# One decoder kernel on one core: expert lists exchanged through TensorE, two norms split over two engines, head and tail of the delta rule reordered

## The chip, the cores and the metric

One core of one Trainium2 chip runs the whole program in one launch. The metric is device time in microseconds; the median of three runs of the kernel before is 2662.2 us (2659.61 to 2668.63). All data are float32 unless said.

## What is computed

A decoder of four layers with three sublayers each, every one followed by a layer norm without weights: `x = layernorm(x + f(x))`, with x of 16 sequences x 128 tokens x 256 channels. The change touches three of the twelve sublayers, one after the other in the program:

```python
# third sublayer (L0 ffn): 16 experts share one matrix; each takes its 128 best tokens
S = softmax(xf @ router_w + router_b)              # xf: 2048 x 256
G, idx = top_k(S.T, 128)
out = xf[idx] @ expert_w + expert_b
y = zeros.at[idx].add(G[..., None] * out)
# fourth (L1 attn): gated delta rule, 8 key and 16 value heads of 128
q, k, v, z = split(x @ w_qkvz.T); b, a = split(x @ w_ba.T)
q, k, v = silu(causal_conv4(q, k, v)); q, k = q/|q|, k/|k|
g = -exp(A_log) * softplus(a + dt_bias); beta = sigmoid(b)
for t in tokens:                                   # S: 128 x 128 per head
    S = S * exp(g[t]); S = S + outer(k[t], (v[t] - k[t] @ S) * beta[t]); o[t] = q[t] @ S / sqrt(128)
y = rmsnorm(o * silu(z)) * norm_weight @ w_out.T
# fifth (L1 xattn): WKV scan over time with k = x and v = ctx, per channel
```

## The kernel before

Tokens of a sequence lie on partitions in `x_tok` [128, 16 batches, 256]; `x_chan` is the same turned, channels on partitions. Each sublayer is a block in which every engine has its own instruction list, run in order; semaphores written by hand tie the lists, and a barrier stands between sublayers. PSUM (`banks`) has 8 banks of 512 columns.

**The end of a sublayer.** `dve_stats` takes statistics of a batch once its sum is added. `dve_norm` (lines 145 to 160) aggregates all 16 batches on VectorE, adds epsilon, lets ScalarE take the root (`act_norm`), inverts, and applies the norm to each batch. `pe_turn_x` transposes it in 8 turns of four 128x128 blocks into banks 0 and 1 by turns; `act_turn_x` copies each turn to `x_chan`. Other sublayers already use `dve_moments`, `act_sqrt`, `dve_invert`, `dve_apply` (lines 170 to 197), which do the same for a part of the batches.

**Expert sublayer, `layer0_ffn`.** 2,048 tokens lie in 8 segments of 256, so partition 16 s + e holds the scores of expert e in segment s. Sixteen rounds of a maximum of eight and a replacement give the 128 best of each segment, sorted, in `best`. SyncE writes them to memory and reads them back so that each partition of an expert holds all eight lists (`lists`); VectorE then merges two lists at a time (larger of one and the reversed other) and sorts again, down to the 128th best, from which the gates follow. Then 16 adds with statistics, and the norm.

**Delta rule, `layer1_delta`.** 16 rounds; round i does key head i // 2 for half of the batches. In a round `unit(n)` is the pair of banks 2n and 2n+1. The head, ahead of the rounds: TensorE projects q, k, v of round 0 (`project`), ScalarE copies (`tap`), VectorE convolves in three steps per channel group u (`convolve`; u = 0, 1 keys and queries, 2, 3 values), ScalarE applies SiLU, the norms of k and q go ln, exp to `lengths`. Two things travel through memory: `lengths` to all partitions (`spread_norms`, 4 writes and one broadcast load of 1 MB into `l1a_sq`) and the rows of the decay (`rows_mem`, two writes and one broadcast load of 1 MB a round into `rows`, part of `ctx_tok`). VectorE scans `rows`, ScalarE takes exp, VectorE weighs with beta (`weigh`), giving `e`. In a round: values turned (`turn_values`), k and q scaled by the norms (`normalise`), key products (`multiply_keys`), times e to `aT` and `att`, inverse of the blocks of 16 (`blk`, through memory, then `invert`), merged by doublings on TensorE (e1, e2, xT1, xT2), `solve`, output `o`, gate with `z` (`gate_project`, `z_out`), norm of o (`gate_norm`), turned output, `project_out`, `add`. The output of round i is finished within round i + 1, that of the last behind the loop, together with the layer norm by halves (`layer_norm`). GpSimd squares the keys and makes `al` from `aT`.

**WKV, `layer1_wkv`.** Two channel halves c; the adds of the second go by quads of four batches with statistics, then the norm as above.

## Time and profile before

| what | value |
|---|---|
| median of three runs | 2662.2 us |
| the profiled execution, whole | 2669.9 us |
| its span | 2668.1 us |
| TensorE, VectorE, ScalarE, GpSimd busy | 82%, 68%, 53%, 13% |
| expert sublayer | 252 to 330 us |
| delta rule | 331 to 385 us with its head until about 390, rounds, tail from 1351 to 1385 us |
| WKV | 1386 to 1484 us |

The span is that of one execution; the runs have no profile. In a timeline a line is a group of like instructions on one engine: start, time in us, engine, line, what is written from what, count, and in brackets how long the engine had been idle before and what ended that. SPq is SyncE issuing a DMA: its time is that of the issue, not of the transfer. PEld is the weight load of a matmul. The granted clock is a share of TensorE's full 2.4 GHz; 0.50 is 1.2 GHz.

### The profile page before, as it was taken

To read this page: it belongs to the slowest core of one execution; us is meant where nothing else is said; L and a number is where in the kernel's file an instruction comes from. 1 tells how busy PE (TensorE), PEld (TensorE's weight loads), DVE (VectorE), ACT (ScalarE), POOL (GpSimd) and SP (SyncE) were. 2 spreads that over 40 slices of the span, in tenths; PEclk is the share of its full clock that TensorE was granted. 3 is DMA by queue.
4 is the path that set the end of the run, shared out by engine and by line. 5 is a ranking of instruction groups with operands and counts; after the bars stand their busy time and mean duration, and the time that the engine had idled before them with its cause. 6 is when DMAs were issued, how large, how long until landed. Compare 5 with 4: busy or idle time off the path is not lost. (4 is left out here: it accounts for less than half of the span.)

```text
span 2668.1 us, 45019 instructions
## 1 busy us (share of the span) xinstructions
PE 2193.6 (82%) x18439; PEld 1684.2 (63%) x18439; DVE 1815.3 (68%) x3155; ACT 1408.4 (53%) x2249; POOL 346.8 (13%) x164
## 2 busy tenths in 40 slices
PE   7986268999999999999851697999999756788855
PEld 4665146777777777777740356999998533455633
DVE  5766657888877778888659534444444878688487
ACT  4654146666666666666535323545455346455347
POOL 0000112222322223222200240000000001100201
PEclk9998678999999999999985899999999877999977
DMA  3000021122122212112221462111100000000000
GB/s 144 2 1 13 15 75 52 53 59 58 49 57 62 79 49 58 51 57 54 45 90 47 151 182 73 44 27 47 36 31 0 5 12 0 11 1 1 17 1 32
DMA packets 159506, 122.82 MB, mean 46 GB/s; under 512 B 117728, under 2 KB 145120, under 8 KB 152800
## 3 DMA queue, kind: packets, MB, share of 16 engines
q1 hardware_dynamic: 156256, 116.00, 14.3%
q0 software_dynamic: 3072, 4.33, 0.9%
q8 instruction: 127, 2.08, 0.3%
q14 instruction: 51, 0.42, 0.1%
HBM read 102.62 MB, written 17.66 MB: 45 GB/s over the span
## 5 line engine op out<-in xcount | busy, mean ns | idle before, releaser
L1543 DVE SCALAR_TENSOR_TENSOR ctx_chan<-l1a_raw,l1a_cw,ctx_chan 128x1024 f32<-128x1024 f32 x192 | 230.8, 1277 | 19.7 <-ACT ctx_chan L1394 18.6
L1156 PE MATMUL banks<-x_chan,l1a_wp 128*128 128x512 f32 x512 | 230.5, 604 | 5.2 <-DMA l1a_wp<-in_l1a_wp_dram 5.2
L1120 POOL TENSOR_TENSOR l1a_sq<-ctx_chan 128x1024 f32<-128x1024 f32 x16 | 152.3, 9516 | 356.4 <-ACT ctx_chan L1398 356.4
L1156 PEld LDWEIGHTS banks<-x_chan,l1a_wp 128*128 128x128 f32 x512 | 98.0, 194 | 117.0 <-issue 110.8
L2644 PE MATMUL banks<-x_chan,more_weights_ahead 128*128 (+1 forms) x1024 | 121.1, 277 | 2.1 <-ACT l2a_ready L2500 2.1
L2644 PEld LDWEIGHTS banks<-x_chan,more_weights_ahead 128*128 128x128 f32 x1024 | 119.5, 194 | 3.8 <-issue 1.6
L1193 PE MATMUL banks<-l1a_wo,l1a_oT 128*128 128x256 f32 x512 | 121.1, 385 | 0.0
L1141 POOL TENSOR_TENSOR l1a_al<-l1a_aT,l1a_outer 128x1024 f32<-128x1024 f32 x32 | 74.8, 2358 | 328.6 <-DVE l1a_aT L1603 328.6
L2664 PE MATMUL banks<-l2a_wo,l2a_oT 128*128 128x256 f32 x512 | 113.2, 379 | 0.0
L1164 PE MATMUL banks<-l1a_wz,x_chan 128*128 128x256 f32 x512 | 113.1, 379 | 0.0
L1164 PEld LDWEIGHTS banks<-l1a_wz,x_chan 128*128 128x128 f32 x512 | 97.2, 190 | 19.6 <-issue 7.2
L1392 ACT ACTIVATE l1a_raw<-banks 128x1024 f32<-128x1024 f32 x64 | 65.5, 1023 | 76.9 <-PE banks L1156 76.8
L2664 PEld LDWEIGHTS banks<-l2a_wo,l2a_oT 128*128 128x128 f32 x512 | 96.1, 190 | 12.4
L1193 PEld LDWEIGHTS banks<-l1a_wo,l1a_oT 128*128 128x128 f32 x512 | 94.7, 190 | 13.7
L2509 ACT ACTIVATE l2a_probs<-l2a_masked,l2a_rowmax 128x128 f32<-128x128 f32 x256 | 98.6, 392 | 3.5 <-DVE l2a_rowmax L2551 3.5
L2547 DVE TENSOR_TENSOR l2a_masked<-banks,l2a_maskf 128x1024 f32<-128x1024 f32 x32 | 39.1, 1220 | 83.2 <-PE banks L2652 83.2
L121 PE MATMUL banks<-ident,x_tok 128*128 128x128 f32 x288 | 50.7, 332 | 53.1 <-DVE x_tok L159 26.5
L2571 DVE COPY l2a_vals<-l2a_ready 128x512 f32<-128x512 f32 x16 | 6.8, 427 | 126.8 <-PE banks L2691 116.1
L1726 DVE TENSOR_TENSOR l1a_vt<-banks,l1a_vt 64x512 f32<-64x512 f32 x64 | 44.5, 695 | 69.3 <-PE banks L1222 69.2
L2521 ACT ACTIVATE l2a_probsT<-banks 128x1024 f32<-128x1024 f32 x32 | 32.7, 1023 | 98.9 <-PE banks L2658 98.9
L142 DVE BATCH_NORM_STATS2 ln_stats_buf<-x_tok 128x6 f32<-128x256 f32 x192 | 75.9, 420 | 9.7 <-ACT x_tok L2831 6.5
L1218 PE MATMUL banks<-l1a_vt,l1a_ec 64*64 64x128 f32 x512 | 70.6, 301 | 13.3 <-ACT l1a_ec L1478 13.3
(624 smaller groups left out, 5766.8 us busy)
## 6 DMA issues: line engine op xcount, KB each, us to landing
ctx_tok<-l1a_rows_mem SPq DMA_DIRECT2D x16, 1024.0 KB, 6.7
l1a_sq<-l1a_norm_mem SPq DMA_DIRECT2D x16, 1024.0 KB, 4.5
ctx_chan<-in_ctxT_dram SPq DMA_DIRECT2D x3, 2048.0 KB, 16.9
l1f_wgu<-in_l1f_wgu_dram SPq DMA_DIRECT2D x4, 1408.0 KB, 11.0
moe_sums<-l1x_zero SPq DMA_DIRECT2D x2, 2176.0 KB, 16.5
ctx_tok<-in_ctx_dram SPq DMA_DIRECT2D x2, 2048.0 KB, 11.4
l1a_wp<-in_l1a_wp_dram SPq DMA_DIRECT2D x8, 512.0 KB, 3.6
l1f_wgu<-moe_sums SPq DMA_DIRECT2D x8, 512.0 KB, 8.2
```

Of the source, the lines that this page charges most:

```text
L142: g.nc.vector.bn_stats(g.stats[:, t, :], g.x[:, t, :]).then_inc(ln_stats, 1)
L1120: P.tensor_tensor(sq[:, 0, :], conv[:, 0, :], conv[:, 0, :], ALU.mult).then_inc(s["k_squared"], 1)
L1141: P.tensor_tensor(heads(al, h), heads(aT, h), bc(outer[:], 1, HALF), ALU.mult).then_inc(s["al_made"], 1)
L1156: mm = MM(ps[:, 2 * (u % 2) + q, :], wp[:, c, u * 128:(u + 1) * 128], g.xT[:, c, t0:t0 + 512], start=c == 0, stop=c == 1)
L1164: mm = MM(unit(h)[:, b * 256:(b + 1) * 256], g.xT[:, c, t0:t0 + S], wz[:, c, :], start=c == 0, stop=c == 1)
L1193: mm = MM(unit(h)[:, b * 256:(b + 1) * 256], oT[:, HALF * h + 2 * b + r, :], wo[:, r, :], start=r == 0, stop=r == 1)
L1218: return MM(quarter(q)[0:64, k, :], xT2[0:64, slot, :], vt[0:64, slot, :], start=True, stop=True)
L1392: A(raw[:, u, :, CONV - 1:], now, ACT.Copy)
L1543: V.scalar_tensor_tensor(t, raw[:, u, :, j:j + S], cw[:, c, j:j + 1], t, ALU.mult, ALU.add).then_inc(s["conv_done" if step == 2 else "conv ...
L2509: ins = A(probs[:, k, :], masked[:, k, :], ACT.Exp, bias=rowmax[:, k:k + 1], scale=128 ** -0.5, accum_out=rsum[:, k:k + 1])
L2644: mm = mm_(next_banks(h)[:, k, :], wq[:, c, h * HALF_HEADS + k, :], g.xT[:, c, bass.ts(i, 128)], start=c == 0, stop=c == 1)
L2664: mm = mm_(ps[:, 6, 0:D], oT[:, h, :], wo[:, h, :], start=h == 0, stop=h == HEADS - 1)
```

## The change

In the experts, `best` is transposed once, copied eight-fold to `wide`, and transposed per segment into banks 4 and 5, which gives every partition all eight lists; ScalarE copies every second list to `odd`, and VectorE merges the others with these from PSUM. In the experts and in WKV the norm is made for batches 0 to 7 while the adds of the others run, and ScalarE applies it (`act_apply`). In the delta rule's head the norms are written ahead of the decay rows and loaded ahead of them; `normalise(0)` comes before the scans; gate projection and z of round 0, and SiLU of the values, come ahead of the decay's exponentials; in round 0 the second half of the convolution comes behind the first inverse product. In its tail the gate and output norm come ahead of the first half's layer norm apply and turns, and the output norm uses root and reciprocal by halves instead of ln and exp.

```diff
-def pe_turn_x(pe, g, ready, turned, turned_out, first=0, stop=None):
+def pe_turn_x(pe, g, ready, turned, turned_out, first=0, stop=None, elsewhere=0):
 
     nc = g.nc
     for n in range(first, stop or TURNS) if g.turn_next else ():
         c, t0 = n % DC, n // DC * GROUP
-        pe.wait_ge(ready, t0 + GROUP)
+        pe.wait_ge(ready, t0 + GROUP - elsewhere)
...
+def dve_lower(v, g, s, shift, t0, t1):
+
+    g.nc.vector.scalar_tensor_tensor(shift[:, t0:t1], g.moments[:, t0:t1, 0], -1.0, g.rstd[:, t0:t1], ALU.mult, ALU.mult).then_inc(s["ln_lowered"], 1)
+
+
+def act_apply(act, g, s, shift, t0, t1):
+
+    act.wait_ge(s["ln_lowered"], 1)
+    for t in range(t0, t1):
+        g.nc.scalar.activation(g.x[:, t, :], g.x[:, t, :], ACT.Identity, bias=shift[:, t:t + 1], scale=g.rstd[:, t:t + 1]).then_inc(s["ln_applied"], 1)
...
-            sp.wait_ge(s["best_made"], 1)
-            sp.dma_start(best_mem.rearrange("e (s k) -> s e k", s=SEGS), best[:]).then_inc(s["best_out"], 16)
-            sp.wait_ge(s["best_out"], 16)
-            sp.dma_start(lists[:].rearrange("p s k -> p (s k)"), bc(best_mem, 0, SEGS)).then_inc(s["lists_in"], 16)
...
+            pe.wait_ge(s["best_made"], 1)
+            pe.wait_ge(s["score_out"], 1)
+            nc.tensor.transpose(ps[:, 2, 0:128], best[:], g.ident[:]).then_inc(s["best_turned"], 1)
+            pe.wait_ge(s["wide_made"], 1)
+            pe.wait_ge(s["expert_out"], B // 2)
+            for n in range(SEGS):
+                mm = nc.tensor.transpose(lists[:, n, :], wide[:, n, :], g.ident[:])
+            mm.then_inc(s["lists_made"], 1)
...
-            pe_turn_x(pe, g, s["ln_out"], s["x_turned"], s["x_turned_out"])
+            pe_turn_x(pe, g, s["ln_applied"], s["x_turned"], s["x_turned_out"], stop=TURNS // 2)
+            pe_turn_x(pe, g, s["ln_out"], s["x_turned"], s["x_turned_out"], first=TURNS // 2, elsewhere=EARLY)
...
-            v.wait_ge(s["lists_in"], 16)
-            merge(sort[0][:], lists[:].rearrange("p (n h) k -> p n h k", h=2))
+            v.wait_ge(s["lists_made"], 1)
+            v.wait_ge(s["odd_out"], 1)
+            link(V.tensor_tensor(sort[0][:], lists[:, 0::2, :], odd[:, :, ::-1], ALU.max))
...
+                if i == EARLY:
+                    dve_moments(v, g, s, 0, EARLY)
+                if i == EARLY + 1:
+                    dve_invert(v, g, s, 0, EARLY, 1)
+                    dve_lower(v, g, s, shift, 0, EARLY)
                 v.wait_ge(s["biased"], i // 2 + 1)
                 at = i % 2 * SEGS + i // 2
                 V.scalar_tensor_tensor(g.x[:, i, :], y[:, i, :], wt[:, at:at + 1], g.x[:, i, :], ALU.mult, ALU.add).then_inc(s["added"], 1)
                 dve_stats(v, g, i, (s["added"], i + 1), s["ln_stats"])
-            dve_norm(v, g, s["ln_stats"], s["ln_mean"], s["ln_sqrt"], s["ln_out"], have_stats=True)
+            dve_moments(v, g, s, EARLY, B)
+            dve_invert(v, g, s, EARLY, B, 2)
+            dve_apply(v, g, s, EARLY, B)
...
-            act_norm(act, g, s["ln_mean"], s["ln_sqrt"])
+            act.wait_ge(s["best_turned"], 1)
+            nc.scalar.activation(wide[:].rearrange("p s (a e) -> p s a e", e=ROUTED),
+                                 bc(ps[:, 2, 0:128].rearrange("p (s e) -> p s e", e=ROUTED), 2, SEGS), ACT.Copy).then_inc(s["wide_made"], 1)
+            act.wait_ge(s["lists_made"], 1)
+            nc.scalar.activation(odd[:], lists[:, 1::2, :], ACT.Copy).then_inc(s["odd_out"], 1)
+            nc.scalar.activation(g.scratch[:], g.ones[:, 0:1], ACT.Sqrt)
+            act_sqrt(act, g, s, 0, EARLY, 1)
+            act_apply(act, g, s, shift, 0, EARLY)
+            act_sqrt(act, g, s, EARLY, B, 2)
...
+            def load_rows(i):
+                k = i // 2
+                sp.dma_start(rows, rows_mem[k, i % 2].rearrange("b n -> (b n)").partition_broadcast(128)).then_inc(s["rows_in"], 16)
+
+            def norms_out(i):
+                sp.wait_ge(s["norm_rs"], i + 1)
+                for j in range(4):
+                    sp.dma_start(norm_mem[j:j + 1, :], lengths[32 * j:32 * j + 1, :]).then_inc(s["norm_out"], 16)
+
+            def norms_in(i):
+                sp.wait_ge(s["norm_out"], 64 * i + 64)
+                sp.dma_start(sq[:].rearrange("p u n -> p (u n)"), norm_mem.rearrange("j n -> (j n)").partition_broadcast(128)).then_inc(s["norm_in"], 16)
+
+            norms_out(0)
             sp.wait_ge(s["rows_begun"], 1)
             for h in range(2):
                 sp.dma_start(rows_mem[:, h], turned[:, h, :]).then_inc(s["rows_out"], 16)
+            norms_in(0)
             sp.wait_ge(s["rows_out"], 32)
...
             load_rows(0)
...
-            spread_norms(0)
...
                 if i + 1 < ROUNDS:
-                    spread_norms(i + 1)
+                    norms_out(i + 1)
+                    norms_in(i + 1)
...
                 for h in range(2):
                     pe.wait_ge(s["silu"], 4 * i + 4)
-                    if h == 0:
+                    if i == 0:
+                        pe.wait_ge(s["z_out"], h + 1)
+                    elif h == 0:
                         pe.wait_ge(s["norm_ln"], i + 1)
                     elif i > 1:
                         pe.wait_ge(s["added"], 2 * i - 2)
-                    elif i:
-                        pe.wait_ge(s["z_out"], 2)
-                    else:
-                        pe.wait_ge(s["tap"], 4)
                     turn_values(h)
...
-                pe.wait_ge(s["wz_loaded"], 16 * (i // 2) + 16)
-                for h in range(2):
-                    if more:
-                        pe.wait_ge(s["tap"], 4 * i + 7 + h)
-                    else:
-                        pe.wait_ge(s["oT_out"], 2 * i - 1 + h)
-                    gate_project(i, h)
+                if i:
+                    pe.wait_ge(s["wz_loaded"], 16 * (i // 2) + 16)
+                    for h in range(2):
+                        if more:
+                            pe.wait_ge(s["tap"], 4 * i + 7 + h)
+                        else:
+                            pe.wait_ge(s["oT_out"], 2 * i - 1 + h)
+                        gate_project(i, h)
...
             pe.wait_ge(s["rest_loaded"], 16 * 4)
+            pe.wait_ge(s["wz_loaded"], 16)
+            pe.wait_ge(s["norm_ln"], 1)
+            pe.wait_ge(s["tap"], 4)
+            for h in range(2):
+                gate_project(0, h)
             for i in range(ROUNDS):
                 round_(i)
             pe.wait_ge(s["added"], 2 * ROUNDS - 2)
-            pe_turn_x(pe, g, s["ln_out"], s["x_turned"], s["x_turned_out"], 0, TURNS // 2)
-            pe.wait_ge(s["x_turned_out"], TURNS // 2)
             for h in range(2):
                 pe.wait_ge(s["normed"], 2 * ROUNDS - 1 + h)
                 turn_output(h)
             for h in range(2):
                 pe.wait_ge(s["oT_out"], 2 * ROUNDS - 1 + h)
                 project_out(h)
+            pe.wait_ge(s["added"], 2 * ROUNDS - 1)
+            pe_turn_x(pe, g, s["ln_out"], s["x_turned"], s["x_turned_out"], 0, TURNS // 2)
             pe.wait_ge(s["added"], 2 * ROUNDS)
             pe_turn_x(pe, g, s["ln_out"], s["x_turned"], s["x_turned_out"], TURNS // 2, TURNS)
 
...
-                for h in range(2):
-                    z_out(i, h)
-                if more:
-                    for u in range(2):
-                        silu(i + 1, u)
+                if i:
+                    for h in range(2):
+                        z_out(i, h)
+                    if more:
+                        for u in range(2):
+                            silu(i + 1, u)
                 act.wait_ge(s["e1_made"], i + 1)
                 A(ec[:], compact(2), ACT.Copy).then_inc(s["e1_out"], 1)
                 act.wait_ge(s["e1T_made"], i + 1)
                 A(ecT[:], compact(3), ACT.Copy).then_inc(s["e1T_out"], 1)
+                if i == 0:
+                    for u in range(2):
+                        silu(1, u)
...
             act.wait_ge(s["gates_turned"], 1)
             A(turned, ps[:, 5, 0:256].rearrange("p (a n) -> p a n", a=2), ACT.Copy).then_inc(s["gates_out"], 1)
             for h in range(2):
-                decay_exp(0, h)
+                z_out(0, h)
             for u in range(2, 4):
                 silu(0, u)
+            for h in range(2):
+                decay_exp(0, h)
             for i in range(ROUNDS):
                 round_(i)
             act.wait_ge(s["ln_mean"], NB + 1)
             A(g.rstd[:, 0:NB], g.rstd[:, 0:NB], ACT.Sqrt).then_inc(s["ln_sqrt"], 1)
-            act_turn_x(act, g, s["x_turned"], s["x_turned_out"], 0, TURNS // 2)
             for h in range(2):
                 square(ROUNDS - 1, h)
-            gate_norm(ROUNDS - 1)
+            for h in range(2):
+                now = slice(HALF * h, HALF * h + HALF)
+                act.wait_ge(s["gsum"], 2 * ROUNDS - 1 + h)
+                A(rs[:, now], ss[:, now], ACT.Sqrt, scale=1.0 / 128, bias=eps[:, 0:1]).then_inc(s["g_rs"], 1)
             for h in range(2):
                 output_turned(ROUNDS - 1, h)
-            A(g.scratch[:], g.ones[:, 0:1], ACT.Sqrt)
+            act_turn_x(act, g, s["x_turned"], s["x_turned_out"], 0, TURNS // 2)
             act.wait_ge(s["ln_mean"], 2 * NB + 3)
             A(g.rstd[:, NB:B], g.rstd[:, NB:B], ACT.Sqrt).then_inc(s["ln_sqrt"], 1)
             act_turn_x(act, g, s["x_turned"], s["x_turned_out"], TURNS // 2, TURNS)
...
             def round_(i):
                 more = i + 1 < ROUNDS
-                for u in range(2):
-                    normalise(i, u)
-                if i:
+                if i:
+                    for u in range(2):
+                        normalise(i, u)
                     for h in range(2):
                         gate(i - 1, h)
                     v.wait_ge(s["al_made"], 2 * i)
...
                 if more:
                     for h in range(2):
                         scan(i + 1, h)
-                    for first in (0, 2):
+                    for first in (0, 2) if i else (0,):
                         for step in range(3):
                             convolve(i + 1, first, step)
                 v.wait_ge(s["e1_out"], i + 1)
                 V.tensor_tensor(p1[:], ec[:], bc(fold[:], 1, VH), ALU.add).then_inc(s["p1_made"], 1)
                 if i:
                     add(i - 1, 0)
+                else:
+                    for step in range(3):
+                        convolve(1, 2, step)
                 v.wait_ge(s["e2_made"], i + 1)
                 V.tensor_tensor(p2[:], compact(2), bc(fold[:], 1, VH), ALU.add).then_inc(s["p2_made"], 1)
                 if more:
...
                 convolve(0, 2, step)
             v.wait_ge(s["rest_loaded"], 16 * 4)
             v.wait_ge(s["zeroed"], 3)
+            for u in range(2):
+                normalise(0, u)
             for h in range(2):
                 scan(0, h)
             for h in range(2):
...
                 round_(i)
             last = ROUNDS - 1
 
-            def layer_norm(half):
+            def layer_norm(half, apply_now):
 
                 done = (NB + 2) * half
                 batches = range(NB * half, NB * half + NB)
...
                 V.tensor_scalar(g.rstd[:, now], g.moments[:, now, 1], 1e-5, None, ALU.add).then_inc(s["ln_mean"], 1)
                 v.wait_ge(s["ln_sqrt"], half + 1)
                 V.reciprocal(g.rstd[:, now], g.rstd[:, now]).then_inc(s["ln_mean"], 1)
-                v.wait_ge(s["ln_mean"], done + NB + 2)
-                for t in batches:
+                if apply_now:
+                    apply(half)
+
+            def apply(half):
+                v.wait_ge(s["ln_mean"], (NB + 2) * half + NB + 2)
+                for t in range(NB * half, NB * half + NB):
                     V.tensor_scalar(g.x[:, t, :], g.x[:, t, :], g.moments[:, t, 0:1], g.rstd[:, t:t + 1],
                                     ALU.subtract, ALU.mult).then_inc(s["ln_out"], 1)
 
-            layer_norm(0)
+            layer_norm(0, False)
             for h in range(2):
                 gate(last, h)
             for h in range(2):
                 sum_gated(last, h)
             for h in range(2):
-                scale_gated(last, h)
+                now = rs[:, HALF * h:HALF * h + HALF]
+                v.wait_ge(s["g_rs"], ROUNDS + h)
+                V.reciprocal(now, now).then_inc(s["g_inverted"], 1)
+                v.wait_ge(s["g_inverted"], h + 1)
+                V.tensor_tensor(heads(go, h), heads(go, h), bc(now, 2, 128), ALU.mult).then_inc(s["normed"], 1)
+            apply(0)
             for h in range(2):
                 add(last, h)
-            layer_norm(1)
+            layer_norm(1, True)
...
+                if n == QUADS + 1:
+                    dve_moments(v, g, s, 0, EARLY)
+                if n == QUADS + 2:
+                    dve_invert(v, g, s, 0, EARLY, 1)
+                    dve_lower(v, g, s, shift, 0, EARLY)
+            dve_moments(v, g, s, EARLY, B)
+            dve_invert(v, g, s, EARLY, B, 2)
+            dve_apply(v, g, s, EARLY, B)
```

## Rows read from the trace of the kernel before

**Rows 1.** The page, part 1: busy time, share of the span, instructions.
```profile
PE 2193.6 (82%) x18439; PEld 1684.2 (63%) x18439; DVE 1815.3 (68%) x3155; ACT 1408.4 (53%) x2249; POOL 346.8 (13%) x164
```

**Rows 2.** Windows, two steady rounds: busy us (count) by engine, granted clock, DMA share.
```profile
456.00:516.00 60.00, 57.58 (x602) 44.66 (x601) 48.83 (x56) 39.63 (x44) 14.49 (x3) 1.00 0.20 54
516.00:576.00 60.00, 57.59 (x595) 45.10 (x594) 47.94 (x55) 38.48 (x44) 15.40 (x4) 0.97 0.22 63
```

**Rows 3.** Timeline, the expert lists by way of memory.
```profile
279.95 0.71 SPq L779 DMA_DIRECT2D l0f_best_mem<-l0f_best  x1
...
289.14 0.69 DVE L868 TENSOR_TENSOR l0f_sort<-l0f_lists 128x512 f32<-128x512 f32 x1 [9.22 <-DMA l0f_lists<-l0f_best_mem]
```

**Rows 4.** The page, part 5, groups: ScalarE copies of 1,024 elements from PSUM.
```profile
L1392 ACT ACTIVATE l1a_raw<-banks 128x1024 f32<-128x1024 f32 x64 | 65.5, 1023 | 76.9 <-PE banks L1156 76.8
```

**Rows 5.** Timeline, the norm behind the experts: aggregation, first turns, last copy.
```profile
319.38 1.15 DVE L152 BATCH_NORM_AGGREGATE ln_moments_buf<-ln_stats_buf 128x2 f32<-128x6 f32 x16
...
322.75 4.39 PE L121 MATMUL banks<-ident,x_tok 128*128 128x128 f32 x20 [17.18 <-DVE x_tok L159]
...
329.41 0.60 ACT L132 ACTIVATE x_chan<-banks 128x512 f32<-128x512 f32 x1 [0.23 <-PE banks L121]
```

**Rows 6.** Timeline: a single ScalarE instruction of 256 elements.
```profile
261.19 0.42 ACT L922 ACTIVATE l0f_lg<-l0f_lg 128x256 f32<-128x256 f32 x1 [0.36 <-DVE l0f_lg L849]
```

**Rows 7.** Timeline, the head of the delta rule, into round 0.
```profile
366.77 1.24 SPq L1050 DMA_DIRECT2D l1a_rows_mem<-ctx_tok  x2
...
369.62 0.34 SPq L1055 DMA_DIRECT2D ctx_tok<-l1a_rows_mem  x1
370.00 1.17 SPq L1061 DMA_DIRECT2D l1a_norm_mem<-l1a_lengths  x4
374.27 4.47 DVE L1598 TENSOR_TENSOR_SCAN l1a_e<-ctx_tok 128x1024 f32<-128x1024 f32 x2 [0.35 <-DMA ctx_tok<-l1a_rows_mem]
...
381.15 2.00 ACT L1398 ACTIVATE ctx_chan<-ctx_chan 128x1024 f32<-128x1024 f32 x2
...
383.25 3.64 PE L1170 MATMUL banks<-ident,ctx_chan 128*128 128x128 f32 x16 [17.11 <-issue]
...
390.92 1.22 DVE L1603 TENSOR_TENSOR l1a_aT<-banks,l1a_e 128x1024 f32<-128x1024 f32 x1 [0.50 <-PE banks L1176]
```

**Rows 8.** Instructions of line 1055, the 16 loads of decay rows: time to landing.
```profile
DMA to landing us min/median/max: 4.5/6.7/8.2
```

**Rows 9.** Timeline, round 0: GpSimd's square of the keys and the last inverse copy.
```profile
417.59 10.03 POOL L1120 TENSOR_TENSOR l1a_sq<-ctx_chan 128x1024 f32<-128x1024 f32 x1 [22.41 <-ACT ctx_chan L1398]
...
434.22 1.01 ACT L1478 ACTIVATE l1a_ec<-banks 128x1024 f32<-128x1024 f32 x1
```

**Rows 10.** Timeline, tail of the delta rule, behind the last round.
```profile
1353.27 2.67 DVE L1756 TENSOR_SCALAR x_tok<-x_tok,ln_moments_buf,ln_rstd_buf 128x256 f32<-128x256 f32 x8
...
1361.64 1.28 ACT L1428 ACT_TABLE_LOAD   x1
...
1363.18 2.36 DVE L1676 TENSOR_TENSOR l1a_go<-l1a_go,l1a_rs 128x1024 f32<-128x1024 f32 x2 [1.90 <-ACT l1a_rs L1428]
1364.55 3.35 PE L1187 MATMUL banks<-ident,l1a_go 128*128 128x128 f32 x16 [7.23 <-DVE l1a_go L1676]
...
1367.74 7.07 PE L1193 MATMUL banks<-l1a_wo,l1a_oT 128*128 128x256 f32 x32
...
1380.26 3.81 PE L121 MATMUL banks<-ident,x_tok 128*128 128x128 f32 x16 [5.45 <-issue]
...
1384.10 0.60 ACT L132 ACTIVATE x_chan<-banks 128x512 f32<-128x512 f32 x1 [0.26 <-PE banks L121]
```

**Rows 11.** Timeline, the norm behind WKV: all 16 applies, the last copy.
```profile
1474.83 5.25 DVE L159 TENSOR_SCALAR x_tok<-x_tok,ln_moments_buf,ln_rstd_buf 128x256 f32<-128x256 f32 x16
...
1482.95 0.60 ACT L132 ACTIVATE x_chan<-banks 128x512 f32<-128x512 f32 x1 [0.22 <-PE banks L121]
```

**Rows 12.** Windows, just behind the gates' transposes of the head.
```profile
366.00:370.00 4.00, 0.14 (x2) 0.00 (x0) 3.34 (x4) 0.62 (x2) 0.00 (x0) 0.67 0.12 33
```

37 lines of the change are left out of this document (18 added, 19 removed).

## Prediction

> **What bounds the kernel now.** I read the page's busy shares first: TensorE is busy 82% of the span [rows 1]. That average hides two kinds of stretch. In the steady rounds of the delta rule TensorE works 57.6 of 60 us [rows 2]; nothing beside it matters there, and the change adds or takes nothing in them. Between the rounds, at the edges of stages, one chain of dependent steps runs through one engine after the other. The change works on five such edges, so I read the timeline of each. At each I ask which step comes last and what comes last once it is moved.
>
> **Edge 1, the expert lists.** The last maximum is out when SyncE issues the write to memory at 279.95, and VectorE merges from 289.14 on [rows 3]: 9.2 us in which nothing else runs. The change puts four steps there. One transpose: 16 take 3.64 us on a TensorE that has been idle [rows 7], 0.23 each, say 0.3 with its start. ScalarE's copy to `wide`, 1,024 elements from PSUM: 1.02, by the copy of that size [rows 4]. Eight transposes: 8 x 0.23 = 1.8. The copy of the odd lists, 512 elements: 0.60, as the copy to `x_chan` [rows 5]. With five hand-overs of 0.12 (an estimate) that is 4.3 us; saved 9.2 - 4.3 = 4.9. Unseen is a ScalarE copy that reads each PSUM value eight times: I take it as dear as any copy of 1,024 outputs, at worst double; at best the hand-overs are nothing. Range 3.8 to 5.3. The sort behind it is the same.
>
> **Edge 2, the norm behind the experts.** Now the 16 adds and statistics end at 319.38, VectorE then applies all 16 batches, TensorE turns from 322.75 (4 transposes a turn, 8 turns), and ScalarE's last copy ends at 329.41 + 0.60 = 330.0 [rows 5]. A split needs VectorE to form moments of eight twice and one small extra product: half of the 1.15 us of [rows 5] plus its 0.2 for the variance is 0.85 more in the middle, plus 0.25 for the reciprocal and 0.2 for `shift`, each by small steps like those. So the adds end 1.3 later, at 320.7; then moments, variance, root and reciprocal of the second half take 1.2, and its apply 8 x 0.33 = 2.6 (16 take 5.25 [rows 11]): done at 324.5 instead of 326.6. ScalarE applies the first half in the meantime: no row shows an Identity of 256 elements with both pointers; an isolated one of that size takes 0.42 [rows 6], eight 3.4, from 314.7 to 318.1, covered by VectorE's adds until 320.7. But ScalarE makes the second root (about 321.6) before its first copy to `x_chan`, so only two turns are done ahead, both waiting in banks 0 and 1. Six remain from 322.3. The eight took 7.3 us from first turn to last copy, 0.73 more for each of the last ones, so six take 5.8: end 328.1, saved 1.9. If Identity needed a table load of its own (1.28, as the load in [rows 10], twice) or TensorE stayed slow, 0.5 would be left; 2.4 at best.
>
> **Edge 3, head of the delta rule.** The order now: ScalarE's exponentials of the decay wait for the scans, the scans for `rows`, and the two SiLU of the values stand behind them at 381.15; so TensorE idles until 383.25, and the second product `aT` ends at 390.92 + 1.22 = 392.15 [rows 7]. From there the block inverse follows at fixed distance (8 DMAs out, one in, the DVE chain). The change moves four things. (a) SyncE writes the norms first: 4 issues, 1.17 us, from about 366.4 on (`norm_rs` is done just before the rows' write of 366.77), then the two of the decay rows (1.24), which therefore start 1.2 later [rows 7]; both loads are broadcasts of 1 MB. The norms' load goes out at about 369.4 and lands in 4.5: 373.9. The rows' load goes at 370.4 instead of 369.62 and shares the queues; such a pair takes 4.5 to 8.2, median 6.7 [rows 8]. That gives 376.5 (374.9 to 378.6) against 374.27 now. This is the cost of the step: +2.2 on the scans. (b) `normalise(0)` comes before the scans: VectorE's taps end at 373.9, the two products (2.35) at 376.3, so they fill the wait that (a) makes. Scans 376.6 to 381.0 (4.47), weighing 381.1 to 383.5 (2.43), both `aT` 2 x 1.23: 386.0. (c) ScalarE's SiLU of the values goes before the decay: TensorE's `gate_project(0)` starts at 366.2, takes 7.07, as the 32 matmuls of its shape in [rows 10], to 373.3, then one z copy, two SiLU, 3.2: 376.5; table load to 377.8, just ahead of the first scan's end at 378.9. (d) TensorE turns values and multiplies keys from 376.6: 1.9 + 3.6 fast, 3.64 + 4.2 slow, that is 382.1 to 384.5, needed at 383.5 and 384.7. So the last arrival is VectorE's, and `aT` ends 6.1 earlier; I take 5.5, for a clock that falls in the middle of (c).
>
> Does it carry? Round 0 before: convolutions filled VectorE until 424.7, `norm_rs` and `xT2` ended with the copy at 434.22 [rows 9]. After: three convolutions of channels 2 and 3 come after `p1`, so the first inverse product is no longer behind them. What is late next is GpSimd's square of the keys, 10.03 us [rows 9], since SiLU of the keys now stands behind both e1 copies and a table load: about 420.4 - 5.5 = 415.0, plus 10.03 = 425.0, sum of squares 426.1, ln, load, exp to 428.8 (0.69 + 1.28 + 0.63), against 434.2: 5.4. So what is won at `aT` is handed on and not more. Range of the edge 3.5 to 6.1.
>
> **Edge 4, tail.** Now layer norm of the first half is applied (2.67 us from 1353.27) and turned ahead of the gate; gated sums, ln with its load, exp with its load, and only then `scale` at 1363.18, turned output at 1364.55, projection at 1367.74 (7.07), then adds, norm, turns from 1380.26 to 1384.10 + 0.60 [rows 10]. After: gate at 1353.3 and 1354.7 instead of 1355.97 on; two squares and two sums by turns of about 1.1 follow, sums end at 1358.3, root and reciprocal by halves without a load, first `scale` ends at 1359.8 instead of 1364.4 and the second at 1361.3: the turned output starts at 1359.9, 4.6 earlier. The apply of the first half (2.67) goes between `scale` and the add, where VectorE now idles 5.9 us for the projection; its four turns go behind the projection, while VectorE makes the second norm (5.4 us); they need 3.2. Cover enough for both. TensorE is then still fast at the last turns, 3.2 instead of the 4.4 of [rows 10]: 1.2 more. Against this, TensorE idles 5.2 us before the turned output and may run the first part of the projection at half speed; the projection used to be fast throughout. I take 0.9 off. 4.6 + 1.2 - 0.9 = 4.9, range 3 to 6. The Trainium skill ("ScalarE: Activation LUTs", section "What ACT_TABLE_LOAD costs") puts a drain of about 1.38 us on top of each table load of 1.28. The row shows the load alone: 1361.64 + 1.28, and the exp at 1362.93 [rows 10]; by the page's price each load taken out would bring 1.38 more, which the trace does not bear out.
>
> **Edge 5, norm behind the WKV stage.** Same edit as edge 2: apply from 1474.83, last copy 1482.95 + 0.60 = 1483.55 [rows 11]. The first half's shift is ready at 1472.2; ScalarE needs until 1475.6 by 0.42 each, which is just where the second root falls (1475.1). Six turns left from 1476.0: 1481.8. Saved 1.8, range 0.5 to 2.3.
>
> **The sum.** 4.9 + 1.9 + 5.5 + 4.9 + 1.8 = 19.0. The profiled execution took 2669.9, so its like would take 2650.9; the median of the runs is 2662.2, so 2643.2. Ends: 11.3 and 22.1 saved, 2650.9 and 2640.1; the runs of before spread over 9 us, half of it goes on each side: 2636 to 2656.
>
> **Rivals.**
> (A) The head gives little. TensorE's grant falls to 0.67 over 366 to 370 [rows 12], just where `gate_project(0)` is put; at half clock throughout it takes 14.1 and ends at 380.3, z and SiLU at 383.5, decay exponentials at 385.9 and 386.9, `aT` at 390.4. Then 1.8 instead of 5.5: 2646.9. For it: TensorE has next to no work from 363 on. Against: it would be busy without a break, and in the tail the projection, begun 3.2 us after TensorE's first work behind an idle of 7.2, took 7.07 for all 32 matmuls, full speed [rows 10]. The Trainium skill ("TensorE: Matmul & The Clock Gate", section "HAM oscillation — how this bites in real kernels") says that bursts behind waits start throttled each time; that is the same case, and here it bears on the start of (c) alone.
> (B) The split norms give nothing: ScalarE's eight applies cost 0.65 each or more, its root comes late, and turns are the bound anyway. Edges 2 and 5 fall to 0.2: 2646.5. For it: eight turns need 7.3 us from 322.75 whatever VectorE does.
> (C) Slower. The rounds are TensorE's, and their grant is 1.00 in some and 0.97 in others [rows 2]; 0.03 of 60 us is at most 1.8 us a round. All edits shift the rounds and take the busy gate projection out of round 0. Lost once more in each of the 14 steady rounds, that is 25.2: 2668.4, and 2672.1 with the loss of A beside it. It decides from 1.4 us a round on. Against it: every wait within a round stays, and TensorE's idle time in a round stays 2.4 us [rows 2].
> (D) The lists do not get faster: TensorE's and ScalarE's steps with repeated reads take the 9.2 us of the DMAs: 2648.1.
>
> **Chances.** Forecast 0.64, A 0.12, B 0.09, D 0.03, C 0.12. About 0.3% (8 us) is what a measurement can tell from no change. The first four all give more than 8; of C I put 0.08 within and 0.04 beyond. Faster 0.88, same 0.08, slower 0.04. The range 2636 to 2656 holds A, B, D and the bounds and leaves out C.
>
> **What would show it.** In the profile after: sort starts 4.3 us behind the last maximum; last `x_chan` copy of the expert stage 7.4 behind its last add and not 10.6; the second `aT` 20.5 us behind the gates' transposes instead of 26; normalise ahead of the scan with the scan waiting for `rows`; turned output 5.3 us behind the last o product instead of 9.9, no ln or exp there. Wrong would be: a z projection with matmuls of twice their length, scans that start after 379, the steady rounds at another period than 60 us, or a stage further on, which no edit touches, of another length.

## The result and the profile after

The changed kernel takes 2647.05 us (median of 6 runs, 2643.63 to 2652.49) against 2665.41 beside it (6 runs, 2659.61 to 2677.86): ratio 0.9927, 95% interval 0.9906 to 0.9948. The profiled execution took 2651.68, its span is 2649.7. 19.0 us had been forecast (2643.2), 18.4 came, in the medians and in the spans of the two profiles.

That agreement is partly luck. By stage in the two profiles, from the first DMA issue of one to that of the next:

| stretch | before | after | difference |
|---|---|---|---|
| ahead of the experts (not edited) | 252.12 | 257.61 | +5.49 |
| experts (edges 1, 2) | 78.73 | 72.36 | -6.37 |
| delta rule (edges 3, 4) | 1055.10 | 1040.69 | -14.41 |
| WKV (edge 5) | 98.49 | 97.31 | -1.18 |
| behind WKV (not edited) | 1183.66 | 1181.73 | -1.93 |

The edited stages give 22.0, 3.0 more than forecast, and stretches that no edit touches take 3.6 back. These stretches move from trace to trace whatever the edit: over the 14 traces of this study (before, after and twelve more, one per kernel) the one ahead of the experts takes 251.95 to 258.30 us and the one behind WKV 1178.4 to 1184.9. In the first, TensorE's clock was at its lower level for 21.3 us in before and 31.5 in after.

Timeline of after, edge 1, which answers to [rows 3]: between the last maximum and the sort stand four steps on two engines.

```profile
285.50 0.48 PE L833 MATMUL banks<-ident,l0f_best 128*128 128x128 f32 x1 [7.14 <-DVE l0f_best L878]
286.01 1.02 ACT L958 ACTIVATE l0f_wide<-banks 128x1024 f32<-128x1024 f32 x1 [7.02 <-PE banks L833]
287.09 1.97 PE L837 MATMUL banks<-ident,l0f_wide 128*128 128x128 f32 x8 [1.11 <-ACT l0f_wide L958]
289.10 0.60 ACT L961 ACTIVATE l0f_odd<-banks 128x512 f32<-128x512 f32 x1 [2.06 <-PE banks L837]
289.80 0.69 DVE L902 TENSOR_TENSOR l0f_sort<-banks,l0f_odd 128x512 f32<-128x512 f32 x1 [4.35 <-ACT l0f_odd L961]
```

From the last maximum to the merge it is 4.35 us instead of 9.22. The copy that reads each value eight times costs 1.02, like any of 1,024 outputs.

Edge 2, answering to [rows 5]:

```profile
315.26 4.04 ACT L189 ACTIVATE x_tok<-x_tok,l0f_shift,ln_rstd_buf 128x256 f32<-128x256 f32 x8 [0.94 <-DVE l0f_shift L182]
317.39 1.97 PE L121 MATMUL banks<-ident,x_tok 128*128 128x128 f32 x8 [11.18 <-ACT x_tok L189]
321.94 0.21 ACT L195 ACTIVATE ln_rstd_buf<-ln_rstd_buf 128x8 f32<-128x8 f32 x1 [2.64 <-DVE ln_rstd_buf L177]
322.78 5.67 PE L121 MATMUL banks<-ident,x_tok 128*128 128x128 f32 x24 [3.42 <-ACT x_chan L132]
328.49 0.60 ACT L132 ACTIVATE x_chan<-banks 128x512 f32<-128x512 f32 x1 [0.26 <-PE banks L121]
```

An apply on ScalarE costs 0.505, not the estimated 0.42. Two turns are made ahead and six remain, 0.9 each. From the first add to the end of the last copy it is 22.63 us instead of 24.19.

Edge 3, answering to [rows 7]:

```profile
365.32 1.16 SPq L1092 DMA_DIRECT2D l1a_norm_mem<-l1a_lengths  x4
366.52 1.33 SPq L1101 DMA_DIRECT2D l1a_rows_mem<-ctx_tok  x2
364.95 8.78 PE L1204 MATMUL banks<-l1a_wz,x_chan 128*128 128x256 f32 x32
372.84 2.36 DVE L1635 SCALAR_TENSOR_TENSOR ctx_chan<-ctx_chan,l1a_sq 128x1024 f32<-128x1024 f32 x2
374.68 1.99 ACT L1442 ACTIVATE ctx_chan<-ctx_chan 128x1024 f32<-128x1024 f32 x2
376.57 4.47 DVE L1650 TENSOR_TENSOR_SCAN l1a_e<-ctx_tok 128x1024 f32<-128x1024 f32 x2 [1.37 <-DMA ctx_tok<-l1a_rows_mem]
380.96 2.44 DVE L1642 TENSOR_TENSOR l1a_e<-l1a_e,l1a_beta 128x1024 f32<-128x1024 f32 x2
383.31 2.35 DVE L1655 TENSOR_TENSOR l1a_aT<-banks,l1a_e 128x1024 f32<-128x1024 f32 x2
```

Normalise fills the wait for the rows and leaves 1.37 of it. From the gates' transposes (364.67; 365.71 in before) to the end of the second aT it is 20.99 us instead of 26.43.

Edge 4, answering to [rows 10]; the last o product starts at 1340.80:

```profile
1349.76 3.28 PE L1227 MATMUL banks<-ident,l1a_go 128*128 128x128 f32 x16 [5.12 <-DVE l1a_go L1830]
1352.88 7.11 PE L1233 MATMUL banks<-l1a_wo,l1a_oT 128*128 128x256 f32 x32
1356.57 1.23 DVE L1733 TENSOR_TENSOR x_tok<-banks,x_tok 128x1024 f32<-128x1024 f32 x1 [3.00 <-PE banks L1233]
1366.84 1.94 PE L121 MATMUL banks<-ident,x_tok 128*128 128x128 f32 x8 [0.16 <-ACT x_chan L132]
1368.81 0.60 ACT L132 ACTIVATE x_chan<-banks 128x512 f32<-128x512 f32 x1 [0.26 <-PE banks L121]
```

From the start of the last o product to the end of the last copy it is 28.6 us instead of 33.9.

Edge 5, answering to [rows 11]:

```profile
1449.17 0.69 DVE L1981 TENSOR_TENSOR x_tok<-x_tok,banks 128x512 f32<-128x512 f32 x1
1456.44 4.04 ACT L189 ACTIVATE x_tok<-x_tok,l1x_shift,ln_rstd_buf 128x256 f32<-128x256 f32 x8 [2.13 <-DVE l1x_shift L182]
1459.02 0.17 DVE L177 TENSOR_SCALAR ln_rstd_buf<-ln_moments_buf 128x8 f32<-128x8 f32 x1
1460.38 0.19 ACT L195 ACTIVATE ln_rstd_buf<-ln_rstd_buf 128x8 f32<-128x8 f32 x1
1460.61 0.20 DVE L201 RECIPROCAL ln_rstd_buf<-ln_rstd_buf 128x8 f32<-128x8 f32 x1 [1.42 <-ACT ln_rstd_buf L195]
1461.20 5.22 PE L121 MATMUL banks<-ident,x_tok 128*128 128x128 f32 x24 [0.67 <-ACT x_chan L132]
1466.45 0.60 ACT L132 ACTIVATE x_chan<-banks 128x512 f32<-128x512 f32 x1 [0.15 <-PE banks L121]
```

The second variance is ready at 1459.19, and its root starts at 1460.38, behind ScalarE's applies: VectorE waits 1.42. From the first add of the second half (1449.17) to the end of the last copy it is 17.88 us. In before it is 18.76, from this line on:

```profile
1464.79 0.69 DVE L1909 TENSOR_TENSOR x_tok<-x_tok,banks 128x512 f32<-128x512 f32 x1
```

Windows of after, three of its 14 steady rounds, each from one first `al` of GpSimd to the next (us, busy by engine, then the granted clock), answering to [rows 2]:

```profile
565.78:627.10 61.32, 58.91 (x602) 46.26 (x601) 48.81 (x55) 39.63 (x45) 14.71 (x4) 0.97 0.19 53
749.74:811.25 61.51, 59.10 (x602) 46.31 (x601) 48.84 (x55) 39.63 (x45) 15.37 (x4) 0.97 0.22 61
811.25:871.13 59.88, 57.47 (x602) 44.58 (x601) 48.81 (x55) 39.63 (x45) 14.70 (x4) 1.00 0.19 54
```

From the third on there are two kinds of round, of about 59.89 and 61.32 us. Before and after have 8 long ones of 14 each, but not the same ones. Inside a long round of after the lost time stands in one place, the multiplies of u (`solve`) behind the copy of xT2:

```profile
607.80:609.80 2.00, 1.24 (x8) 0.80 (x7) 1.14 (x1) 1.53 (x2) 0.00 (x0) 1.00 0.01 3
609.80:611.80 2.00, 2.00 (x27) 1.95 (x26) 0.09 (x1) 1.01 (x2) 0.00 (x0) 1.00 0.12 50
611.80:613.80 2.00, 2.00 (x26) 2.00 (x24) 0.69 (x1) 0.76 (x2) 0.00 (x0) 0.51 0.98 414
613.80:615.80 2.00, 2.00 (x29) 2.00 (x26) 0.81 (x2) 0.91 (x2) 0.00 (x0) 0.64 1.03 434
```

TensorE waits 0.76 us for that copy (607.8 to 609.8), and from 611.83 to 615.25 the clock is at the lower of its two levels, 1.2 GHz; the 0.64 is the mean of a window that it leaves in part. Price: 61.32 - 59.89 = 1.43 us. The same is found in every long round of the eight kernels that leave this wait as it is: 41 falls, one a round, each 3.4 us long, and each begins 2.4 to 2.8 us behind the end of the copy of xT2. A wait of 0.85 us ahead of the turned output, in every round too, has no fall behind it; so the length of a wait alone doesn't decide.

### The profile page after: what moved, and what is told of

Its sections match the earlier page's. It is cut to its first block and busy times, and to the rows that moved or that the text cites. A ratio compares the mean times of both kernels' runs of the same rounds, so it can differ in the third digit from the quotient of the medians.

```text
span 2649.7 us, 45005 instructions
## 1 busy us (share of the span) xinstructions
PE 2198.2 (83%) x18407; PEld 1693.0 (64%) x18448; DVE 1812.2 (68%) x3147; ACT 1414.4 (53%) x2265; POOL 338.8 (13%) x164
## 5 line engine op out<-in xcount | busy, mean ns | idle before, releaser
L1160 POOL TENSOR_TENSOR l1a_sq<-ctx_chan 128x1024 f32<-128x1024 f32 x16 | 144.3, 9019 | 360.4 <-ACT ctx_chan L1442 360.4
L121 PEld LDWEIGHTS banks<-ident,x_tok 128*128 128x128 f32 x288 | 43.4, 182 | 55.1 <-ACT x_tok L189 19.6
```

Of the source, the lines that this page charges most:

```text
L121: mm = nc.tensor.transpose(g.ps[:, n % 2, t * 128:(t + 1) * 128], g.x[:, t0 + t, c * 128:(c + 1) * 128], g.ident[:])
L1160: P.tensor_tensor(sq[:, 0, :], conv[:, 0, :], conv[:, 0, :], ALU.mult).then_inc(s["k_squared"], 1)
```

## The experiments

**Each part undone alone.** Four kernels, one part put back in each. First the lists:

```diff
+            sp.dma_start(best_mem.rearrange("e (s k) -> s e k", s=SEGS), best[:]).then_inc(s["best_out"], 16)
...
+            sp.dma_start(lists[:].rearrange("p s k -> p (s k)"), bc(best_mem, 0, SEGS)).then_inc(s["lists_in"], 16)
...
-            nc.tensor.transpose(ps[:, 2, 0:128], best[:], g.ident[:]).then_inc(s["best_turned"], 1)
```

> The kernel after, with the expert lists sent through memory again; the rest of it untouched. Theory (each edge has its own price, and the traces of before and after show it): the sort starts 9.2 us behind the last maximum instead of 4.35, the expert stage is 4.9 us longer, the whole kernel 4.9. Rival (what is won at one edge is partly made by the others, through the clock or the phase of the rounds): another number, by more than 1 us, in the total of the four runs of this kind, whose single losses by the traces are 4.9, 2.8, 8.7 and 5.3, sum 21.7.

The norms (the same in both stages), the head, the tail:

```diff
-            act_sqrt(act, g, s, 0, EARLY, 1)
-            act_apply(act, g, s, shift, 0, EARLY)
-            act_sqrt(act, g, s, EARLY, B, 2)
+            act_norm(act, g, s["ln_mean"], s["ln_sqrt"])
```

> The kernel after, with both split layer norms (behind the experts, behind WKV) made whole again on VectorE. Theory: first residual add to last x_chan copy 1.6 us longer in the expert stage (24.2 instead of 22.6), 1.2 us longer in the WKV stage, 2.8 in all. Rival B of the prediction (turns bound both anyway): at most 0.4 in all.

```diff
-            norms_out(0)
             sp.wait_ge(s["rows_begun"], 1)
...
-            for h in range(2):
-                gate_project(0, h)
...
-            for u in range(2):
-                normalise(0, u)
```

> The kernel after, with the head of the delta rule as before: decay rows ahead of the norms on SyncE, gate_project(0) and z in round 0, decay exponentials ahead of the SiLU of the values, normalise(0) behind the scans, all convolutions of round 1 ahead of p1. Theory 1 (the prediction's: what is won at aT is handed on and not more): second aT 5.4 us later, and the multiply by al of round 1 5.4 us later too. Theory 2 (the traces of before and after: 24.8 against 19.9 us from the gates' transposes to the first al, 90.1 against 81.3 to that of round 1): round 0 itself is 3.9 us longer as well, of which 2.8 us lie behind the copy of xT2, where TensorE multiplies at half clock for 9 us instead of 4; 8.7 us in all. GpSimd's square of the keys in round 0 is back at 10.0 us.

```diff
-                A(rs[:, now], ss[:, now], ACT.Sqrt, scale=1.0 / 128, bias=eps[:, 0:1]).then_inc(s["g_rs"], 1)
+            gate_norm(ROUNDS - 1)
...
-            layer_norm(0, False)
+            layer_norm(0, True)
```

> The kernel after, with the tail of the delta rule as before: the first half's norm applied and turned ahead of the gate, gate norm by ln and exp for both halves. Theory: from the multiply by al of the last round to the last x_chan copy 5.3 us longer; granted clock of the output projection 1.00 in both. Rival: the four turns that are hidden behind the projection were hidden before too, then only the two table loads and the pair of ln and exp count, 3.9 us (2 x 1.28 and 2 x 0.65).

Measured as whole kernels: 2647.95 (2641.93 to 2652.72, 6 runs), 2651.06 (2639.57 to 2657.78, 7), 2649.62 (2635.78 to 2655.36, 7) and 2647.21 us (2643.50 to 2652.60, 5). The kernel before beside them took 2661.2; the ratios are 0.9942 [0.9916, 0.9969], 0.9945 [0.9920, 0.9970], 0.9933 [0.9908, 0.9958] and 0.9934 [0.9908, 0.9959]. None can be told from after (0.9927), though by the traces each lacks 3 to 6 us of the gain. The ratios lose 4.0, 4.8, 1.6 and 1.9 us against after, 12 in all, where the expectation of the lists had 21.7; its rival, another number by more than 1 us, is met by that, but each ratio is only known to 7 us, so the totals decide neither. A likely reason is in the traces: their long rounds are 2, 4, 8 and 3 of 14, against 8 in after, and six long rounds fewer are 8.6 us, more than any part is worth. (Each trace is of one run, so the long rounds of the other runs aren't known.) So totals can't price one part here; stretches of the trace can. Over all 14 traces:

| part | with it | without it | worth | forecast |
|---|---|---|---|---|
| lists: last maximum to sort | 4.34 to 4.35 (12 traces) | 9.22, 9.12 | 4.8 | 4.9 |
| norm: sort to start of delta | 39.71 to 40.18 (10), mean 40.0 | 41.71, 41.74 | 1.7 | 1.9 |
| head: start of delta to first al | 53.6 to 55.7 (11, without rows_first), mean 54.5 | 59.66, 58.71 | 4.7 | 5.5 |
| tail: last o product to last copy | 28.61 to 30.61 (12), mean 29.8 | 33.92, 33.89 | 4.1 | 4.9 |
| norm behind WKV: first add of the second half to last copy | 17.69 to 18.16 (10), mean 17.9 | 18.76, 18.88 | 0.9 | 1.8 |

Both norms of best1 and best2 are left out, since they split otherwise. gate_late counts as with the head's part, though it lacks the gate projection there. To the 16.2 of the table comes round 0, below, with 1.3: 17.5. The expectations of u_norms and u_tail are answered by the same rows. The norms are worth 1.7 and 0.9, not the 0.4 of the rival. In the tail the turned output starts 8.96 us behind the o product instead of 13.77, 4.8 earlier, more than the rival's 3.9 for table loads with ln and exp alone; so the moved apply and turns count too. That the projection stays at full clock, also expected, did not hold: it takes up to 8.32 us instead of 7.07.

The expectation for the head had two theories. From the first al to the end of the copy of xT2, round 0 takes 43.4 to 43.8 us in the eleven kernels whose convolutions of channels 2 and 3 stand behind p1 and whose gate projection is at the head, 44.73 in before and 45.08 in u_head: 1.3 of real gain. From there to the next al it takes 16.33, 17.77, about 19.2 or about 20.5 us, steps of about 1.4, with before at 20.56, after at 17.77 and u_head at 16.33. In these four the lower clock is granted for 0, 3.4, 6.8 and 9.6 to 10.2 us of the stretch. Theory 2, that these 2.8 us belong to the change, falls: u_head has none of them. They are falls of the clock as in the steady rounds.

**Two steps of the head.** The order of SyncE alone, and the gate projection (with its z and the SiLU of the next keys) alone:

```diff
-            norms_out(0)
             sp.wait_ge(s["rows_begun"], 1)
...
-            norms_in(0)
             sp.wait_ge(s["rows_out"], 32)
             load_rows(0)
+            norms_out(0)
+            norms_in(0)
```

> The kernel after, with the decay rows ahead of the norms on SyncE in the first round, nothing else changed. Theory (prediction, step a): the rows land 2.2 us earlier (the scans could start at the normalise's end or before), but the norms land later, as in before at 376.9 by the time of that profile, normalise(0) stands ahead of the scans on VectorE and now waits for the norms; so the second aT ends 1 to 4 us later than in after (delta start to first al 55.5 to 58.5 instead of 54.6). Rival: both loads end together anyway, 54.6 within 0.5.

```diff
-            for h in range(2):
-                gate_project(0, h)
             for i in range(ROUNDS):
                 round_(i)
```

> The kernel after, with the gate projection of round 0, its z and the two SiLU of round 1 back inside round 0. Theory: ScalarE has the SiLU of the values done before the decay either way, so the first al comes at the same 54.6 us behind delta's start, or up to 1.7 later if TensorE turns the values colder; round 0 gets the 7.1 us of gate projection back and is 2 to 4 us longer than the 60.0 to 62.9 of the kernels that have it outside. Rival A of the prediction (the gate projection at half clock is what holds the head): the first al comes 1.5 us or more EARLIER.

rows_first: the first al comes 58.60 us behind delta's start, 4.0 later than in after, where 1 to 4 were expected. Its timeline:

```profile
366.03 0.34 SPq L1087 DMA_DIRECT2D ctx_tok<-l1a_rows_mem  x1
366.41 1.17 SPq L1092 DMA_DIRECT2D l1a_norm_mem<-l1a_lengths  x4
371.14 0.34 SPq L1096 DMA_DIRECT2D l1a_sq<-l1a_norm_mem  x1
375.86 2.36 DVE L1635 SCALAR_TENSOR_TENSOR ctx_chan<-ctx_chan,l1a_sq 128x1024 f32<-128x1024 f32 x2 [5.60 <-DMA l1a_sq<-l1a_norm_mem]
378.14 4.46 DVE L1650 TENSOR_TENSOR_SCAN l1a_e<-ctx_tok 128x1024 f32<-128x1024 f32 x2
```

The four small writes of the norms (2 KB) stand behind the 1 MB load of the rows: from the end of the last issue at 367.58 it is 3.6 us until the load goes, and 4.6 more until it lands; VectorE waits 5.60. With the norms first, the same step is 1.4 us at most (366.48 to 367.89), and the rows' load lands 7.1 us behind its issue instead of 4.6. So normalise ahead of the scans is worth little without the norms ahead on SyncE: 58.60 against 59.66 and 58.71 with the whole head as before.

gate_late: the first al comes at 53.74 (after: 54.64). 0.8 of the 0.9 are the load of the rows: from its issue to the scan it is 6.3 instead of 7.1 us; from scan to first aT both take 6.74. So in the changed kernel the moved gate projection, 8.78 us and partly at half clock, isn't what holds the head, against rival A, which wanted 1.5 or more here. Whether it lengthens the load of the rows isn't shown by one trace. Round 0 takes 44.23 and 20.37 us, together 64.60, 3.2 more than in after; 2.6 of that are falls of the clock.

**The wait ahead of u filled.** If the wait of 0.76 us is needed for the fall of the clock, filling it should end the long rounds. The two fillers compute 128 and 256 columns of an output block twice, with the same result.

```diff
+                if i:
+                    for n in range(1):
+                        for r in range(2):
+                            MM(unit(1)[:, 0:128], oT[:, HALF + r, :], wo[:, r, 0:128], start=r == 0, stop=r == 1)
                 previous_out(1, 2, 4)
                 solve(i)
```

> The kernel after, with two matmuls more per round (128x128 by 128, the first half of a column block of the output projection computed twice, same result) in the 0.76 us in which TensorE waits for the copy of xT2. They take about 0.5 us and fit in the wait. Theory W (the rounds of 61.3 us, 8 of 14 in the profile of after, are those in which the grant falls to half for 3.4 us in the multiplies of u, behind that wait; each costs 1.43): with the wait filled the falls become fewer, down to none, rounds 59.9, up to 11.4 us less than the profile of after. Rival X (the grant falls because of the 64-row multiplies or the broadcast load that starts there, whatever the wait): 2 to 8 such rounds, as in the five profiles so far, and no gain in the median.

> The same with the whole column block computed twice: two matmuls of 256 columns, 1.0 us, of which 0.24 go beyond the wait, 3.4 us over 14 rounds. Theory W: no round of 61.3 us is left, rounds of 60.1. Rival X: 2 to 8 long rounds as before, and 3.4 us more.

fill128: 2640.86 us (2639.56 to 2641.43, 4 runs), ratio 0.9912 [0.9882, 0.9941]. fill256: 2639.30 (2635.27 to 2647.41, 4), 0.9900 [0.9868, 0.9932]. Windows of fill128, two rounds:

```profile
563.98:623.86 59.88, 57.91 (x606) 45.02 (x605) 48.80 (x55) 40.38 (x45) 14.70 (x3) 1.00 0.20 54
623.86:683.75 59.89, 57.92 (x606) 45.04 (x605) 48.72 (x55) 39.26 (x45) 15.39 (x4) 1.00 0.22 63
```

In the eight kernels without filler 41 of 112 steady rounds are long by the clock (2 to 8 of 14), in the six with filler none of 84. For the rounds theory W holds and rival X falls. 41/8 x 1.43 = 7.3 us on the mean, and the medians lie 6 to 8 below that of after; but by the ratios to the kernel before it is 4 and 7, with intervals that overlap after's. A round of fill256 costs 59.93, 0.04 more and not 0.24. The Trainium skill ("TensorE: Matmul & The Clock Gate", section "HAM oscillation — how this bites in real kernels") describes falls of the clock behind DMA waits of 3 to 5 us between bursts. The trace agrees that a fall follows a wait, but here it is one of 0.76 us.

**GpSimd's square.** In round 0 of after it took 2.05 us instead of 10.03 [rows 9], and VectorE's six convolutions beside it 8.90 instead of the 7.26 that they take in gate_late, where no square runs beside them.

```profile
412.44 8.90 DVE L1595 SCALAR_TENSOR_TENSOR ctx_chan<-l1a_raw,l1a_cw,ctx_chan 128x1024 f32<-128x1024 f32 x6
415.81 2.05 POOL L1160 TENSOR_TENSOR l1a_sq<-ctx_chan 128x1024 f32<-128x1024 f32 x1 [26.52 <-ACT ctx_chan L1442]
```

The kernel fill128 with a memset ahead of the square, longer from round to round, shifts its start against VectorE's instructions:

```diff
                 pool.wait_ge(s["silu"], 4 * i + 1)
+                if i:
+                    P.memset(pause[:, 0:34 * i], 0.0)
                 P.tensor_tensor(sq[:, 0, :], conv[:, 0, :], conv[:, 0, :], ALU.mult)
```

> The kernel fill128, with one GpSimd memset more per round, of 34 to 510 columns (0.1 to about 0.5 us, longer from round to round), between the SiLU of the keys and their square, so that the square asks at another phase of VectorE's back-to-back instructions (1.2 us each) every round. Theory (both engines share a way into SBUF, and who has it keeps it): in some rounds the square takes 2.0 to 2.2 us and one VectorE convolution beside it 2.9 instead of 1.25; in the others 10.03 as always; nothing between, or only where VectorE pauses. Rival (10.03 is what this square costs beside any VectorE work): 10.03 in every steady round. The rounds stay 59.9 either way, TensorE's being the bound.

Neither came. In the steady rounds the squares took 9.63, then 9.91, 9.88, 9.85 and so on down to 9.56, shorter by what they started later: their end is fixed. One of them, and VectorE beside it:

```profile
833.20 9.77 POOL L1163 TENSOR_TENSOR l1a_sq<-ctx_chan 128x1024 f32<-128x1024 f32 x1
841.14 1.21 DVE L1740 TENSOR_TENSOR x_tok<-banks,x_tok 128x1024 f32<-128x1024 f32 x1
```

It ends at 842.97, 1.83 us behind the start of VectorE's first instruction with an input from PSUM; undisturbed the square takes 1.89. All 14 steady squares of this kernel, and those of before, after and fill128, end 1.83 or 1.84 behind such a start. So a square did next to nothing for 8 us behind VectorE's scalar-tensor-tensor and tensor-tensor instructions on SBUF, and then it ran. The Trainium skill ("GPSIMD Engine Reference", section "1. Specifications") says that the two engines share their SBUF interfaces, with contention when VectorE has two SBUF inputs; the trace agrees. What lets the square in between in round 0 (1.9 to 2.2 us in ten traces with VectorE at work, 5.87 in u_tail) stays open, but the starts sort the cases. In the ten the square starts 0.06 to 0.39 us ahead of VectorE's next instruction; in u_tail it is 0.45, in before and u_head 1.07. The memsets moved it only from 1.07 to between 0.96 and 0.61, so this experiment never reached the phase of round 0, and its theory is not refuted. One round of this kernel is long (61.20) at a granted clock of 1.00, for another reason: VectorE's normalise waits 3.82 us for the load of the norms, and TensorE 0.93 behind it.

**Towards a faster kernel.** best1 is fill128 with round 0's waits filled too (12 matmuls ahead of the product xT2, shown, and 3 ahead of u), and the split at 4 batches for ScalarE. best2 is best1 with filler ahead of the turns of both norms. filled is best1 with the split at 8 again:

```diff
+                    for n in range(12):
+                        MM(unit(1)[:, 0:256], g.xT[:, 0, 0:128], wz[:, 0, :], start=True, stop=True)
...
-        EARLY = B // 2
+        EARLY = 4
```

> The kernel fill128, with TensorE's waits of round 0 filled too (12 matmuls of 256 columns ahead of the product xT2, 3 ahead of u, results not used), and with 4 instead of 8 batches of the two split norms on ScalarE (VectorE applies 12). Theory for round 0: no half clock behind xT2, first al to second 58.7 to 60 instead of 61.4 to 61.6. Theory for the norms (ScalarE's 8 applies of 0.505 each hold back its second root, and VectorE waits 1.4 us for it behind WKV): the second root comes 1.2 us earlier, the last x_chan copy 0.5 to 1.2 earlier in each of the two. Rival: TensorE at half clock bounds the six last turns (5.2 us), nothing gained, or lost where VectorE's 12 applies come too late.

```diff
+            pe.wait_ge(s["added"], 14)
+            for n in range(8):
+                nc.tensor.matmul(ps[:, 3, 0:256], g.ident[:], ew[:, 0, :], start=True, stop=True)
             pe_turn_x(pe, g, s["ln_applied"], s["x_turned"], s["x_turned_out"], stop=AHEAD)
```

> The kernel best1, with matmuls whose results are not used ahead of the turns of both norms (8 ahead and 8 between behind the experts, 10 and 2 behind WKV), so that TensorE is not idle for 7 to 11 us before them. Theory: the last turns run at full clock, 0.5 instead of 0.9 us each; the copies of 0.6 us then bound them; 1 to 1.5 us less at each norm. Rival: the grant does not rise in time (turns of 0.9 us as before) and the filler delays the second turns by up to 1 us each. The whole: 2640.9 us of fill128 less 1.5 for round 0, 1.5 for the norms and 2.5 for this, 2635; by the rivals 2641 to 2643.

```diff
-        EARLY = 4
+        EARLY = B // 2
```

> The kernel fill128 with TensorE's waits of round 0 filled as in best1, the norms as in after (8 and 8). Theory W: no half clock behind any copy of xT2: 16.3 us from the copy of xT2 to the first al of round 1 (16.3 to 20.6 in the kernels without it), all 14 rounds 59.9 but the first two; the whole 1.4 to 2.9 us below the 2640.9 of fill128, 2639, and its runs within 4 us of each other. Rival: the spread of the runs comes from elsewhere (the stages behind, whose waits are not filled): runs spread over 8 us or more, median 2641 to 2645.

best1: one run, 2638.66. Round 0 takes 59.81, as expected. The norms take 40.63 and 17.84 by the table's rows, against means of 40.0 and 17.9, nothing gained. The second root comes at once (VectorE waits 0.28 for it behind WKV, not 1.42), but the third turn now waits for VectorE's first four applies and starts 11.96 us behind the first add instead of 12.03; the six turns take 5.06 and 5.24 us (5.67 and 5.22 in after), mostly at half clock. best2: 2644.61 (2639.64 to 2646.74, 6), 0.9921 [0.9892, 0.9950], each of its runs above best1's one. Its timeline behind the experts:

```profile
318.65 6.46 PE L850 MATMUL banks<-l0f_ew,ident 128*128 128x256 f32 x16 [12.55 <-DVE x_tok L939]
324.94 1.04 PE L121 MATMUL banks<-ident,x_tok 128*128 128x128 f32 x8
325.82 3.62 PE L853 MATMUL banks<-l0f_ew,ident 128*128 128x256 f32 x16
329.27 1.04 PE L121 MATMUL banks<-ident,x_tok 128*128 128x128 f32 x8
330.65 1.12 PE L121 MATMUL banks<-ident,x_tok 128*128 128x128 f32 x8 [0.34 <-ACT x_chan L132]
```

The turns are fast now, a pair each 1.4 us instead of 1.8, as the theory had it. But the filler waits for the 14th add and starts at 318.65. A filler of 256 columns counts as two matmuls of 0.4 at half clock, so eight take 6.46, and the first turns, whose batches are applied by 313.5, wait until 324.94: the edge is 4.4 longer than in best1. Behind WKV, with less filler, it is 0.7 shorter (17.11).

filled: 2640.65 us (2638.23 to 2646.94, 6 runs), ratio 0.9901 [0.9873, 0.9929]. No long round, 16.34 behind xT2 in round 0, as expected. But the median is that of fill128 within its spread, and the runs spread over 8.7 us, as the rival had it; those of fill256 spread over 12.1. So much of the spread comes from elsewhere than these rounds, the rival says from stages whose waits are not filled, which no run shows. The kernels with filler have the lowest medians of the study, 6 to 8 us below the changed kernel, but their intervals overlap with its; that one of them beats it is likely by the rounds and not shown by the totals.

## Why the prediction was right, and where not

**The sum.** 19.0 forecast, 17.5 by the stretches of 14 traces, 18.4 in the medians. Every edge came within a us of its term. Rivals B and D are refuted by the table (B's own sum, 0.2 for 3.7, gives 2646.7 and not 2646.5). Of the 22.0 of the two profiles, 2.8 lie behind xT2 in round 0, where the clock was low for 3.4 us in after and for 10.2 in before; u_head, without the edit, has none of that. What the unedited stretches took back, 3.6, lies within their scatter of 6 us each. So that the 18.4 meets the 19.0 this well is luck in part. Two of the forecast's own signs of being wrong came, steady rounds of another period than 60 us and an unedited stage of another length, and mean nothing here: both differ from trace to trace.

**Edge 1** came to 0.1 us. The two copies took 1.02 and 0.60, as forecast; the transposes took 0.48 and 1.97 for 0.3 and 1.8, and the five hand-overs 0.3 in all instead of 0.6, which makes up for it.

**Edge 2** is 0.2 below its term. The root was in time here; the mis-sized term is the six turns. They took 6.31 us from the first of them to the last copy, and not 5.8: the 0.73 a turn of [rows 5] includes fast ones at the end, and in after the clock was low until 328.53. The last copy came 8.4 us behind the last add, where 7.4 was to be seen. (Half of 1.15 plus 0.2 is 0.78, not 0.85.)

**Edge 5** is worth half its term, 0.9 for 1.8. The six turns took 5.85, as forecast, but started 12.03 us behind the first add where the forecast's times put them at 11.2. One half of these 0.8 is ScalarE's apply: 0.42 by an isolated instruction of its size [rows 6], 0.505 measured, 4.04 for eight. The other half is what stands between the applies and the third turn, the root and a copy of 0.60 that frees a bank: 0.82, for which 0.4 was allowed. best1 shows that a root in time alone gives nothing, at least where VectorE has to apply the next batches first. Rival B had named the late root and the turns as bound; it was wrong in the size.

**Edge 3** is worth 4.7 at the first al plus 1.3 up to xT2, 6.0, against 5.5. The order of steps came as forecast, with normalise in the wait. Everything in after's profile stands 1.04 us earlier than in before's, by the gates' transposes, so times are compared from there: the scan came at 11.9 for 10.9, the end of aT at 20.99 for 20.3. The mis-sized term is the load of the rows, 7.1 from issue to landing and not 6.1. The gate projection took 8.78 for 7.07, but gate_late shows that it wasn't what came last. **One step failed:** "What is late next is GpSimd's square of the keys, 10.03 us". It took 2.05, and the next to be late was the copy of xT1 behind ScalarE's SiLU of the values (420.17, 2.25 us), which waited for VectorE's convolutions now behind p1, lengthened by the square. The saving at xT2, 5.4 forecast, was 5.94 in that profile from the gates' transposes on; a nearly right number from a wrong chain, that is luck. The duration of an instruction had been carried over without asking what it did in those 10 us.

**Edge 4**: the turned output starts 8.96 behind the o product instead of 13.77, so 4.8 for the forecast 4.6. What was set against it, 0.9 for half clock in part, is about what happens: the turned output's transposes take 0.2 more on the mean and the projection 0.6 more, 7.07 to 8.32 us in the twelve traces. The mis-sized term is the 1.2 for fast last turns: 0.5 came in four of the twelve traces and nothing in the other eight, 0.16 on the mean. In the profile of after, one of the two luckiest, the edge is 5.3; the mean is 4.1.

**Rival C** had the right mechanism, a round that is longer by a fall of the clock, at 1.43 us where it allowed for at most 1.8, and the wrong condition: there are 8 long rounds in before as in after, and 2 to 8 in the eight kernels with this wait. That the wait ahead of u must be there is shown; what picks the round is not. As there is one trace of each kernel, it isn't shown either that the picking goes by the run and not by the edit (u_head has its long rounds in the same eight places as before, gate_late and rows_first share their four). The runs of one kernel speak for the run: the mean granted clock of after's six goes from 0.914 to 0.920, with the lowest values in its two slowest. These falls are a part of the measurement's spread, 9 to 20 us in the kernels without filler, and they were the largest thing found to gain.

## What to carry to other kernels

Where TensorE bounds, compare the lengths of like rounds first: two values with different granted clock are a gain to be had by half a microsecond of filler in the right wait, and until then a part of the noise that hides any edit of a few us. Price small edits by stretches of the trace over several runs, not by the total. Filler must fit the wait at the slow clock; a little too much costs more than the clock gives back.

## What the runs showed of the hardware

- Two elementwise engines on SBUF: GpSimd stood 8 us behind VectorE's back-to-back instructions and ran in its full 1.83 us as soon as one of them read from PSUM. It got in where it started 0.06 to 0.39 us ahead of VectorE's next instruction (ten traces) and not from 0.45 on; VectorE then paid 1.64 us in one instruction, 2.92 instead of 1.28.
- A load that waits for four writes of 2 KB, issued just behind a broadcast load of 1 MB, went 3.6 us behind the last issue's end and landed 4.6 later; with the writes issued ahead of the broadcast, it went 1.4 us behind the last issue (366.48 to 367.89).
- One stretch of TensorE (round 0 behind the copy of xT2) took 16.33, 17.77, about 19.2 or about 20.5 us in fourteen traces, with the lower clock granted for 0, 3.4, 6.8 and 9.6 to 10.2 us of it.
- In 41 of 41 long rounds the fall of the clock began 2.4 to 2.8 us behind a wait of 0.76 us; behind a wait of 0.85 us elsewhere in the same rounds there was none.
